# Moving a convolution, a residual sum and a gate's product to other slots of a hand-written schedule

## The reference, cut to what matters

```python
# block 1: a Mamba mixer and an FFN
h = layernorm(x, ln1_g, ln1_b)
h = h + mamba_mixer(rmsnorm(h, rms_w), ...)
x = x + h
x = x + (relu(layernorm(x, ln2_g, ln2_b) @ ffn_w1 + ffn_b1) @ ffn_w2 + ffn_b2)

# mamba_mixer
xi, z = split(x @ in_proj_w)
xc = silu(causal_conv(xi, conv_w) + conv_b)            # 4 taps
dbc = xc @ x_proj_w                                    # dt (64), B (16), C (16)
delta = softplus(dbc[..., :64] @ dt_proj_w + dt_proj_b)
h_t = exp(delta * A) * h_{t-1} + (delta * xc) * B      # over 512 tokens, 16 states
y = (sum over states of h_t * C + D_param * xc) * silu(z)
return y @ out_proj_w

# block 2: a gated recurrence over the 8 sequences (64 x 64 in the reference's view)
ft = sigmoid(xt @ wf.T + c @ uf.T + bf)
it = sigmoid(xt @ wi.T + c @ ui.T + bi)
gt = tanh(xt @ wc.T + c @ uc.T + bc)                   # the candidate gate, "gc"
c = ft * c + it * gt
h = tanh(x @ wo.T + c_final @ uo.T + bo)
```

## Time and profile before

| | us |
|---|---|
| median of 3 runs | 1798.81 |
| lowest, highest | 1788.87, 1801.2 |
| the profiled execution | 1799.12 |
| its span | 1797.3 |

### The profile page before, as it was taken

How to read it: one execution, slowest core, us unless ns; L and a number is a source line. 1 busy time by engine, 2 the same in 40 slices (tenths; PEclk the granted TensorE clock), 3 DMA queues, 4 the chain that set the end, 5 groups by cost and what they waited for, 6 DMA issues and landing times.

```text
span 1797.3 us, 17168 instructions
## 1 busy us (share of the span) xinstructions
PE 1433.0 (80%) x5520; PEld 673.4 (37%) x5520; DVE 1249.9 (70%) x1908; ACT 846.6 (47%) x1442; POOL 654.7 (36%) x337
## 2 busy tenths in 40 slices
PE   2324669899897979799936889999898989999973
PEld 1102244545354545454522224343433334343341
DVE  2399898989989898870147786767777666666125
ACT  3553747565565655533110454445454545444522
POOL 3475858566666655721332121203030302000001
PEclk9656789999898989899966889999999999999997
DMA  5414151515142232300324342313242322220027
GB/s 161 165 37 175 37 187 49 187 49 185 51 140 97 95 120 92 129 24 12 94 58 88 67 111 65 84 49 86 52 104 49 91 63 67 65 49 2 25 72 232
DMA packets 95896, 160.12 MB, mean 89 GB/s; under 512 B 8656, under 2 KB 76816, under 8 KB 92688
## 3 DMA queue, kind: packets, MB, share of 16 engines
q1 hardware_dynamic: 95808, 159.04, 30.4%
HBM read 111.95 MB, written 47.05 MB: 88 GB/s over the span
## 4 chain that ended last, share of the span: by engine, by line
PE 60%; DVE 22%; ACT 7%; issue 7%; POOL 3%; DMA 2%; SPq 0%; DVEq 0%; ACTq 0%; POOLq 0%
PE psum L910 23%; PE psum L1710 9%; PE psum L1646 7%; PE psum L1595 6%; PE psum L1620 5%; PE psum L1635 5%; DVE psum L507 5%; DVE mx L1210 4%; PE psum L955 2%; DVE stats L1188 1%; DVE middle L473 1%; PE psum L905 1%; ACT psum L693 1%; ACT front L612 1%; PE psum L1590 1%
## 5 line engine op out<-in xcount | busy, mean ns | idle before, releaser
L1210 DVE TENSOR_REDUCE mx<-psum 128x1 f32<-128x512 f32 x512 | 340.8, 686 | 183.4 <-PE psum L1620 181.2
L1423 ACT ACTIVATE pw<-psum 128x512 f32<-128x512 f32 x512 | 298.7, 597 | 359.4 <-PE psum L1635 358.8
L851 POOL TENSOR_TENSOR hb<-ddb,bcb 128x1024 f32<-128x1024 f32 x128 | 301.4, 2371 | 134.2 <-DMA ddb<-dd 59.5
L507 DVE TENSOR_TENSOR_SCAN psum<-psum,hb 128x512 f32<-128x512 f32 x224 | 261.8, 1214 | 57.9 <-ACT psum L693 37.5
L1620 PE MATMUL psum<-kp,qp 96*128 96x512 bf16 x512 | 208.9, 410 | 79.9 <-DVE mx L1210 58.8
L693 ACT ACTIVATE psum<-ddb,A_neg 128x512 f32<-128x512 f32 x256 | 164.6, 679 | 94.7 <-DVE hb L510 53.2
L1635 PE MATMUL psum<-qp,kp 99*128 99x512 bf16 x512 | 201.0, 395 | 2.9 <-ACT pw L1423 1.9
L1530 POOL TENSOR_TENSOR rstd<-rstd,neg_half 128x4 f32<-128x4 f32 x16 | 16.3, 1017 | 469.2 <-DVE rstd L1195 469.2
L1646 PE MATMUL psum<-pw,v_sb 128*32 128x512 f32 x1024 | 143.8, 635 | 3.1 <-ACT pw L1423 2.5
L510 DVE TENSOR_TENSOR hb<-psum,bcb 128x1024 f32<-128x1024 f32 x112 | 137.2, 1225 | 3.9
L1620 PEld LDWEIGHTS psum<-kp,qp 96*128 96x128 bf16 x512 | 51.1, 100 | 204.6 <-DVE mx L1210 114.7
(11 more groups left out here) (172 smaller groups left out, 2148.3 us busy)
## 6 DMA issues: line engine op xcount, KB each, us to landing
ddb<-dd SPq DMA_DIRECT2D x64, 512.0 KB, 7.8
bcb<-bc SPq DMA_DIRECT2D x32, 512.0 KB, 6.2
parts<-parts_sb SPq DMA_DIRECT2D x96, 128.0 KB
dd<-dd_out SPq DMA_DIRECT2D x8, 1024.0 KB, 4.1
qp<-parts SPq DMA_DIRECT2D x32, 256.0 KB, 7.9
kp<-parts SPq DMA_DIRECT2D x16, 384.0 KB, 4.6
x_front<-x_dram SPq DMA_DIRECT2D x8, 512.0 KB, 3.9
xh<-x_front SPq DMA_DIRECT2D x8, 512.0 KB, 5.1
```

Of the source, the lines that this page charges most:

```text
L507: e.tensor_tensor_scan(to[:, g, :], a[:, g, :], h[:, g, :], 0.0, ALU.mult, ALU.add).then_inc(scan_ok, 1)
L851: e.tensor_tensor(hb[n % NHB], ddb[k % NSLOT][:, 1:2, :].to_broadcast([P, 2, L]), bcb[q][:, 0, :, :], ALU.mult).then_inc(bx_ok, 1)
L1210: used.up(e.tensor_reduce(mx[u % 2][:, n:n + 1], bank(used.n % 2), AXIS.X, ALU.max))
L1423: e.activation(pw[n % NPW], bank(5 + n % 2), ACT.Exp, scale=HD ** -0.5).then_inc(exp_ok, 1)
```

## The change

Three things move; no operation is added, removed or resized.

1. VectorE: the convolution's halves go from slots 1 and 2 to slots 0 and 1, `back_sum` from slot 2 to slot 1, behind the convolution of half 1. GpSimd's order waits follow (slots 0 and 1).
2. TensorE: the product of the candidate gate goes from behind `sums(i, 1)` to directly behind the product for z; the ring's list follows, so the uses behind it take other banks.
3. The readers of that product follow: `gate_c` goes on ScalarE from slot 11 to slot 5, between `mid_z` and `mid_tz`; `gate_in` on VectorE from slot 11 to slot 5.

```diff
@@ -78,6 +78,8 @@
             use("act", "gi", i - 2, 2)
         if mid:
             use("act", "z", i + 1, 2)
+        if gate:
+            use("dve", "gc", i - 2, 2)
         if back:
             use("act", "bturn", i - 1, 2)
         if mid:
@@ -88,8 +90,6 @@
             use("act", "dt", i + 1, 2)
         if back:
             use("act", "ffn4", i - 1, 4)
-        if gate:
-            use("dve", "gc", i - 2, 2)
         if back:
             use("dve", "ffn_out", i - 1, 2)
         if gate:
@@ -566,14 +566,16 @@
                         scan(i, u)
                     if u == 0 and back:
                         gated(i - 1, 1)
-                    if u == 2 and back:
+                    if u in (0, 1) and mid:
+                        conv(i + 1, u)
+                    if u == 1 and back:
                         back_sum(i - 1)
-                    if u in (1, 2) and mid:
-                        conv(i + 1, u - 1)
                     if u == 3 and back:
                         back_moments(i - 1)
                     if u == 4 and mid:
                         mid_xc(i + 1)
+                    if u == 5 and gate:
+                        gate_in(i - 2)
                     if u == 6 and mid:
                         mid_sz(i + 1)
                     if u == 6 and front:
@@ -582,8 +584,6 @@
                         mid_soft(i + 1)
                     if u == 11 and s:
                         gated(i, 0)
-                    if u == 11 and gate:
-                        gate_in(i - 2)
                     if u == 12 and front:
                         front_square(i + 2)
                     if u == 14 and back:
@@ -768,6 +768,9 @@
                         back_apply(i - 1)
                     if u == 5 and mid:
                         mid_z(i + 1)
+                    if u == 5 and gate:
+                        gate_c(i - 2)
+                    if u == 5 and mid:
                         mid_tz(i + 1)
                     if u == 6 and back:
                         back_turned(i - 1)
@@ -788,8 +791,6 @@
                     if u == 9 and back:
                         back_relu(i - 1, 6)
                         back_relu(i - 1, 7)
-                    if u == 11 and gate:
-                        gate_c(i - 2)
                     if u == 11 and front:
                         front_square(i + 2)
                     if u == 13 and front:
@@ -871,8 +872,8 @@
                     for u in range(AHEAD):
                         bx(i, u)
                 for u in range(NUNIT):
-                    if u in (1, 2) and mid:
-                        e.wait_ge(conv_ok, 2 * (i + 1) + u)
+                    if u in (0, 1) and mid:
+                        e.wait_ge(conv_ok, 2 * (i + 1) + u + 1)
                     if u == 3 and back:
                         norm_power(0, b_var, i, b_rstd)
                     if u == 4 and mid:
@@ -1021,6 +1022,8 @@
                     gate_one(i - 2, "gi", 1)
                 if mid:
                     mid_in(i + 1, "z", 1)
+                if gate:
+                    gate_one(i - 2, "gc", 2)
                 if back:
                     back_turn(i - 1)
                 if mid:
@@ -1037,8 +1040,6 @@
                         back_first(i - 1, c)
                 if s:
                     sums(i, 1)
-                if gate:
-                    gate_one(i - 2, "gc", 2)
                 if back:
                     back_second(i - 1, 0)
                 if s:
```

## The result

| | before | after |
|---|---|---|
| median, us | 1800.01 (4 runs) | 1819.63 (4 runs) |
| lowest to highest, us | 1788.87 to 1807.5 | 1813.31 to 1825.0 |
| profiled execution, us | 1799.12 | 1813.31 |
| its span, us | 1797.3 | 1811.5 |

What follows compares the result with a forecast made beforehand. Neither VectorE nor TensorE alone bounds it; TensorE's work between back_sum and the FFN delays VectorE in slot 10. 2.4 + 21.5 - 4.3 - 4.9 = +14.7 us gave 1813.5 us, range 1796 to 1822.

Steps and rivals of the forecast that it cites:

- The chain: Full pass, back_sum through x_proj and FFN to slot 10's decay: x_proj and that decay come 7.2 us later.
- 0.2 us of saved bank waits: TensorE before x_proj: bank waits that change hands were estimated to take 0.2 us off the delay.
- VectorE's wait in slot 5: At gate_in in a full pass: VectorE stands for 7.3 us until the candidate gate's tanh, instead of 1.15.
- The collision: Moved convolution against GpSimd's third product: costs the rest of one product, 2.35 us per pass.
- rival A: Load lands outside the convolution or costs only its head: no clash, 1798.1 us; chance 0.18.
- the arrival of the load: DMA for GpSimd's third product: lands 5.1 to 6.6 us into the pass, inside the convolution's 4.9 to 7.7.
- the forget gate's wait of 1.31 us: VectorE behind slot 10 waits for the forget gate's tanh; this 1.31 us was counted as saved.
- My term of 2.9 us: VectorE from slot 10 to gate_state: saves gate_in's 1.2 us and waits of 0.41 and 1.31 us.
- rival B: TensorE's clock halves in the new 6 us wait before back_second: +6.6 us, 1820.1 us; chance 0.22.
- 1.5 us of room: Before the forget gate sets the end, the FFN's output was given about 1.5 us of room.
- Passes 7 and 8: Passes without a middle: the gate's product fills TensorE's wait for back_apply, saving 4.3 and 4.9 us.
- Rival C: Slot 10's 4.53 us wait absorbs what slot 5 adds, its decay not moving: 1777.6 us; chance 0.04.

Runs made afterwards that it cites:

- The half product: Changed kernel, with the candidate gate's product leaving out its two state terms (8 of 16 instructions) in passes 2 to 6; ratio 0.9997 to the kernel before.
- the kernel without a collision: Changed kernel, with GpSimd's third and fourth products each waiting for one half of the convolution; ratio 1.0039 to the kernel before.

## Why the prediction was right, point by point

**The chain was the right one.** With the forecast of pass 5 counted from its first scan, and what was measured: back_sum at 16.4 us, measured 15.98; x_proj at 43.7, measured 43.8; the decay of slot 10 at 65.5, measured 65.5; gate_state at 97.1, measured 97.7. The half product and gate_in in slot 9 show causes and not only times: cutting the product gives back at least its length, taking VectorE's wait away gives back little. The first three points agree better than the terms behind them. back_sum came 0.1 us later than before and not 0.5; from back_sum to x_proj it took 7.2 us more than before and not 6.7, because the product of 6.9 us brought no 0.2 us of saved bank waits and the output product ran 0.3 us longer (6.55 instead of 6.24). That these two cancel at x_proj is luck.

**VectorE's wait in slot 5** was forecast at 7.3 us and measured at 7.74. That it costs little beside the chain was worked out through the wait of slot 10, and the kernel with gate_in in slot 9 shows it.

**The collision** came in every pass from 0 to 6, and rival A is refuted; taking it away was worth 13.5 us. Its price was set a little high: 12.4 us in sum, forecast 15.4 (1.3 + 6 x 2.35). The step that failed here is the arrival of the load. I had it 5.1 to 6.6 us into the pass; in passes 3 to 6 it came at 4.3 to 4.7. Two things were wrong. I let the pass begin 1.2 us closer behind the last product hC of the pass before; passes 3, 4 and 6 began 0.6 us closer (3.50 us instead of 4.12) and pass 5 not at all. And the load came 7.8 to 8.9 us behind the end of that hC, where it had taken 8.0 to 9.5 before; why isn't shown. GpSimd in pass 5:

```profile
556.66 2.35 POOL L852 TENSOR_TENSOR hb<-ddb,bcb 128x1024 f32<-128x1024 f32 x1 [6.39 <-DMA ddb<-dd]
```

GpSimd started 0.17 us ahead of the convolution, so in passes 3 to 6 the first instruction waited (1.5 to 1.9 us), not one in the middle. Only in passes 1 and 2 did it hit the middle (2.1 and 2.2). The Trainium skill (SBUF — State Buffer, section SBUF: two separate sides) says that whichever of the two starts first keeps the port pair for its whole instruction; both patterns fit that, and the kernel without a collision shows 2.87 us for each half. The same section counts a VectorE instruction in a 2-port perf mode as well as one with two SBUF inputs. The instruction that waited in passes 3 to 6 (L470) reads one tensor only, so it can fall under the rule by its mode alone; no run shows in which mode it ran.

**Why the pass did not begin earlier.** I took the forget gate's wait of 1.31 us as gone. It is 0.69 us in passes 2, 3 and 5 and 1.30 in pass 4, and the passes with a front grew by 4.1 to 4.9 us instead of 4.3. What keeps the wait is a second chain that my sum left out. In both traces it is 16.70 us from the start of the pass's last sums over states (L955, L956) to gate_state, in every one of passes 2 to 6. The sums need VectorE's gated product (L519). Before the change they began 2.5 us behind its end (3.0 in pass 6); in passes 2, 3 and 5 of the changed kernel TensorE waits for it (0.29 us in pass 5) and begins 0.15 us behind it. So it is 16.84 us from the gated product to gate_state, of which VectorE's own queue fills all but 0.69. In pass 4 the sums begin 0.93 us behind it, and the wait is 1.30 us. My term of 2.9 us for this stretch measured 2.3.

Half of rival B came: the clock stands at 0.50 when back_second begins. But I priced it wrongly: the slow first half hides behind VectorE's gated product, which the kernel with the extra matmuls showed by undoing it. (The price has a slip in its working too: 3.4 us less 1.5 us of room is 1.9, not 1.65.)

**Passes 7 and 8** were forecast at -4.3 and -4.9 and measured at -5.0 and -4.4. TensorE of the changed kernel shows the gate's product where the wait for back_apply was: in pass 7 the sums are back at 1.92 us, and the 32 instructions of the FFN in pass 8 run at full rate behind 1.24 us of waiting; a new wait of 0.78 us for the last relu takes back a part there.

```profile
778.35 1.92 PE L956 MATMUL psum<-hb,sel 128*32 128x512 f32 x16
780.88 14.00 PE L911 MATMUL psum<-back,w 128*128 128x512 f32 x32 [0.61 <-ACT back L709]
...
851.05 14.00 PE L911 MATMUL psum<-back,w 128*128 128x512 f32 x32 [1.24 <-ACT back L709]
```

**Rival C**, the wait of slot 10 swallowing that of slot 5, is refuted by the 4.31 us that remain in slot 10. The sum was 14.7 us, the measured growth of D 15.8 us: passes 0 and 1 gave 2.4 of 2.4, passes 2 to 6 22.5 of 21.5, passes 7 to 9 -9.1 of -9.2. That pass 3 would grow more and pass 2 less than the others did not show (4.7 and 4.9 us). The median lies 6 us above the point; one trace of each kernel can't say in which phase.

## What to carry to other kernels

When an engine's queue has several waits in a row, look for the last one that the same chain causes, and count a moved operation there, not at the wait where it first shows: 7.7 us of VectorE standing still cost under 1 us per pass on average, 6.9 us of TensorE ahead of x_proj were paid in full. A move that loses in the full passes can win in the last ones, where the pipeline runs empty; put it only there. And before moving an instruction, check on the other engine's timeline what it will run beside: a place of 2.8 us was free in one order and cost 1.5 to 2 us in the next.

## What the runs showed of the hardware that I had not expected

The same four VectorE instructions (128x512, float32, SBUF to SBUF) took 2.87 us alone and up to 5.1 us beside one GpSimd product of 2.35 us. In each case seen, the instruction that was held up waited for 0.2 to 0.3 us less than the rest of that product. It works the other way too: with the convolution alone moved, the product of GpSimd that began during a convolution instruction of pass 1 took 2.88 us instead of 2.35. Keeping TensorE busy with extra matmuls did hold the granted clock at 1.00 over a stretch where it had been 0.50, and the kernel became slower by 3.6 us in D. The Trainium skill (TensorE: Matmul & The Clock Gate, section Part 1: The HAM clock gate (the "warmup" mystery)) describes the return to half rate behind idleness; the runs agree (0.50 behind 6.2 us of waiting, and behind 2.19 us in the kernel with the extra matmuls). Here the higher clock was worth nothing where TensorE then had to wait for VectorE, and its loss cost 1.6 us per pass where VectorE waited for TensorE.
